# A transformer of two attentions and two expert layers on one core: routing moved ahead, blocks interleaved, the band mask moved from TensorE to VectorE

## The reference

```python
# attention A: 16 heads of 128, a band of 64 keys
h = x * rsqrt(mean(x*x) + eps) * norm_w
Q, K, V = (h @ W.T + h @ A.T @ B.T / 16 for each)      # then rope on Q and K
scores = Q @ K.T                                        # scaled; keys outside the band: -1e30
x = x + lora(softmax(scores) @ V)
# expert layer, run twice (f after attention A, g after attention B)
logits = z @ gate_w.T                                   # 16 experts
top4 = the 4 largest, weights by softmax over them
x = x + shared_mlp(z) + sum over the 4 of weight * expert_mlp(z)   # silu(z@wg.T)*(z@wu.T) @ wd.T
```

## Time and profile before

| | us |
|---|---|
| median of three runs | 1501.32 (1501.03 to 1511.45) |
| the profiled execution | 1505.28 |
| its span, first to last instruction | 1503.4 |
| PE busy | 1312.6 (87%) |
| DVE busy | 1045.4 (70%) |
| POOL busy | 870.6 (58%) |
| ACT busy | 847.9 (56%) |

### The profile page before, as it was taken

One profiled execution on the slowest core, in us unless ns is written; L12 is line 12 of the kernel. 1 busy time (PEld: TensorE's weight loads), 2 busy tenths in 40 slices (PEclk: granted clock), 3 DMA queues, 4 the chain that ended last, 5 costly groups with the idle time before them and its releaser, 6 DMA issues.

```text
span 1503.4 us, 28392 instructions
## 1 busy us (share of the span) xinstructions
PE 1312.6 (87%) x8194; PEld 1101.2 (73%) x8194; DVE 1045.4 (70%) x2274; ACT 847.9 (56%) x2102; POOL 870.6 (58%) x764
## 2 busy tenths in 40 slices
PE   5999999999988983749998989899999999978982
PEld 3888888888877883538777767677777778867872
DVE  5666666646777544438888878688888886777544
ACT  1444444454435542238778777677878875436541
POOL 3555555540346774247878777678778650356772
PEclk9999999999979997769999999999999999979996
DMA  3000000001326336221222221122222202326335
GB/s 112 26 26 26 27 25 25 16 9 55 122 84 204 109 103 213 52 58 29 59 59 63 55 68 43 43 61 63 57 69 56 57 1 77 121 92 196 103 103 178
DMA packets 58253, 110.60 MB, mean 74 GB/s; under 512 B 11456, under 2 KB 29440, under 8 KB 57856
## 3 DMA queue, kind: packets, MB, share of 16 engines
q1 hardware_dynamic: 46976, 82.11, 19.3%
q0 software_dynamic: 9024, 24.65, 5.4%
q10 hardware_dynamic: 2112, 2.10, 0.4%
HBM read 63.99 MB, written 15.47 MB: 53 GB/s over the span
## 4 chain that ended last, share of the span: by engine, by line
PE 45%; issue 19%; POOL 17%; DVE 11%; DMA 3%; ACT 2%; SPq 0%; POOLq 0%; DVEq 0%; ACTq 0%
PE ps L1450 31%; PE ps L1596 7%; POOL pb_odd L1089 4%; POOL yt L1089 3%; POOL rb L1074 2%; PE ps L1813 2%; POOL z L1089 2%; PE ps L1538 2%; POOL pb_low L1089 2%; POOL ra L1078 2%; DVE x_res L840 1%; PE ps L1673 1%; DVE pt_lo L902 1%; PE ps L1701 1%; DVE rb L541 1%
## 5 line engine op out<-in xcount | busy, mean ns | idle before, releaser
L902 DVE TENSOR_TENSOR pt_lo<-ps,pt_hi 128x512 fp32r<-128x512 f32 (+3 forms) x384 | 205.6, 548 | 54.8 <-ACT pt_hi L1369 48.4
L1450 PE MATMUL ps<-kh,qh 128*128 128x512 f32 (+3 forms) x768 | 204.1, 376 | 22.3 <-DMA qh<-qt_hi 10.2
L887 DVE TENSOR_REDUCE nmb<-ps 128x1 f32<-128x1024 f32 (+7 forms) x256 | 191.8, 749 | 29.1 <-PE ps L1450 28.1
L1369 ACT CAST pt_hi<-ps 128x512 fp32r<-128x512 f32 (+3 forms) x384 | 178.5, 481 | 58.7 <-PE ps L1813 53.1
L1450 PEld LDWEIGHTS ps<-kh,qh 128*128 128x128 f32 x768 | 132.3, 196 | 46.2 <-issue 14.3
L1450 PE MATMUL ps<-pt_hi,vst 128*128 128x512 f32 (+3 forms) x384 | 157.0, 409 | 0.9 <-DVE ra L867 0.8
L1450 PE MATMUL ps<-pt_lo,vst 128*128 128x512 f32 (+3 forms) x384 | 132.9, 350 | 0.0
L994 POOL TENSOR_TENSOR pa<-pa,rinv 128x384 f32<-128x384 f32 x64 | 52.9, 827 | 134.5 <-DVE rinv L581 134.5
L1167 ACT ACTIVATE pa<-ps,nmax 128x192 f32<-128x192 f32 x128 | 53.1, 423 | 131.0 <-DVE nmax L575 131.0
L1029 POOL DMA_INDIRECT xg<-zbuf,gidx x94 | 97.6, 1039 | 41.3 <-issue 23.8
L1089 POOL TENSOR_TENSOR pb_odd<-pb_odd,rib 128x1024 f32<-128x1024 f32 (+1 forms) x64 | 105.3, 1670 | 21.9 <-DVE rib L894 21.3
(11 more groups left out here) (222 smaller groups left out, 4219.9 us busy)
## 6 DMA issues: line engine op xcount, KB each, us to landing
raw_w<-in_wx SPq DMA_DIRECT2D x36, 608.0 KB
rb<-raw SPq DMA_DIRECT2D x192, 64.0 KB, 2.0
yg<-ybuf SPq DMA_DIRECT2D x16, 512.0 KB, 4.9
qh<-qt_hi SPq DMA_DIRECT2D x64, 128.0 KB, 2.3
qh<-qt_lo SPq DMA_DIRECT2D x64, 128.0 KB, 2.4
wa<-in_wa SPq DMA_DIRECT2D x16, 384.0 KB, 3.0
wb<-in_wb SPq DMA_DIRECT2D x8, 384.0 KB, 3.4
wo_a<-in_wo_a SPq DMA_DIRECT2D x16, 128.0 KB, 2.0
```

The costliest lines, as they stand in the source:

```text
L887: v.tensor_reduce(nmb[:, par, i:i + 1], ps[:, b:b + 2, :].rearrange("p b k -> p (b k)")[:, 0:P * (t + 1)], AX.X, ALU.max, negate=True).the ...
L902: v.tensor_tensor(pt_lo[:, s % 3, at], ps[:, 4 + s % 2, at], pt_hi[:, s % 3, at].bitcast(F32), ALU.subtract).then_inc(sem("b_pt_lo"), 1)
L1369: s_.copy(pt_hi[:, s % 3, at], ps[:, 4 + s % 2, at]).then_inc(sem("b_pt_hi"), 1)
L1450: return t_.matmul(o, l, r, start=start, stop=stop)
```

## The change

In attention A the mask matmuls go. DVE adds the mask with the maximum: for each tile one operation computes minus (scores + mask) into a new SBUF buffer `sma` and the minimum of it into `nmax`. The exponential reads `sma` with scale -1. The scores of a head's first pairs now wait for the maximum before them, no longer for the exponential.

In the expert layer the routing is issued earlier. The first norm and `logits(0)` move forward into the output projection, and `picked(0)` to its step 14. The later pieces follow two to three blocks earlier. The order of the blocks becomes: 12 shared, r0, r1, two shared, r2, r3, two shared, the rest. The conversions shift accordingly, and POOL has one fewer.

The rows of `ybuf` are laid out so that a token's four outputs are contiguous; four DMAs of two tiles each read all of it into a `yg` that holds all eight tiles. In f a conversion of attention B's value weights moves from among the additions to before them.

```diff
+FRONT = 12
+ORDER = ([("s", n) for n in range(FRONT)] + [("r", 0), ("r", 1), ("s", 12), ("s", 13), ("r", 2), ("r", 3), ("s", 14), ("s", 15)] +
+         [("r", b) for b in range(4, NB)])
-POOL_LO = 9
+POOL_LO = 8
-YG_RING = 4
+TILE_ROWS = TOPK * P + TOPK
...
-                for t in range(NT):
-                    if t >= YG_RING:
-                        sp.wait_ge(sem(f"{s}_added"), since(s, "added") + t - YG_RING + 1)
-                    first = P * (1 + TOPK * t)
-                    sp.dma_start(yg[:, t % YG_RING, :, :],
-                                 ybuf[first:first + TOPK * P, :].rearrange("(k p) e -> p k e", p=P)).then_inc(
-                        sem(f"{s}_yl{t % YG_RING}"), 16)
+                for n in range(NT // 2):
+                    sp.dma_start(yg[:, 2 * n:2 * n + 2, :],
+                                 tiles[2 * n:2 * n + 2, 0:TOPK * P, :].rearrange("t (p k) e -> p t (k e)", k=TOPK)).then_inc(
+                        sem(f"{s}_yl{n}"), 16)
...
-                v.tensor_reduce(nmax[:, 2 * n:2 * n + 2], ps[:, bank, 0:2 * KW].rearrange("p (t k) -> p t k", t=2),
-                                AX.X, ALU.max, negate=True).then_inc(sem("a_max"), 1)
+                v.memset(waited[:, :], 0.0)
+                for m in range(2):
+                    t = 2 * n + m
+                    last = v.tensor_tensor_reduce(out=sma[:, t, :], in0=ps[:, bank, KW * m:KW * m + KW],
+                                                  in1=maska[:, 0 if t == 0 else 1, :], scale=-1.0, scalar=3e38,
+                                                  op0=ALU.add, op1=ALU.min, accum_out=nmax[:, t:t + 1])
+                last.then_inc(sem("a_max"), 1)
...
                 step(0)
                 normalized(s, 1)
-                picked(0)
                 step(1)
                 norm_lo(s, 1, ACC[before][1])
                 step(2)
+                picked(s, 1)
                 step(3)
-                picked(1)
+                starts()
+                places()
+                step(4)
+                hot(0)
+                step(5)
+                hot(1)
+                step(6)
+                experts()
+                tables()
                 shifted()
...
-                    s_.activation(pa[:, t, 0:KW], ps[:, bank, KW * m:KW * m + KW], ACT.Exp,
+                    s_.activation(pa[:, t, 0:KW], sma[:, t, :], ACT.Exp, bias=nmax[:, t:t + 1], scale=-1.0,
...
                 if n < 2:
-                    after(pe, "a_exp", 4 * h + n - 1)
+                    after(pe, "a_max", 4 * h + n - 1)
...
-                    mm(o, qr[:, u, P * t:P * t + P], kr[:, u, P * t:P * t + KW], True, False)
-                    last = mm(o, idb[:, :], maska[:, 0 if t == 0 else 1, :], False, True)
+                    last = mm(o, qr[:, u, P * t:P * t + P], kr[:, u, P * t:P * t + KW])
...
-                    if h == 10:
+                    if h == 7:
                         norm(nxt, 0, 0)
+                    elif h == 11:
+                        logits(nxt, 0)
...
-ACT_HI = {0: (2,), 2: (3,), 4: (4,), 5: (5,), 7: (6,), 8: (7,), 10: (8,), 11: (9,), 13: (10,), 14: (11,),
+ACT_HI = {0: (2,), 2: (3,), 4: (4,), 6: (5,), 8: (6,), 9: (7,), 12: (8,), 14: (9,), 16: (10,), 17: (11,),
...
-DVE_LO = {12: (9,), 14: (10,), 15: (11,), 17: (12,), 19: (13,), 21: (14,), 23: (15,), 25: (16,), 27: (17,)}
+DVE_LO = {13: (8,), 15: (9,), 17: (10,), 18: (11,), 20: (12,), 21: (13,), 23: (14,), 24: (15,), 26: (16,), 27: (17,)}
```

More of the change, by code:

```diff
@@ L100, in build @@
             topf = sb("topf", [P, NT, 8], c=own)
+            ie = sb("ie", [P, NE], c=own)
             ex = sb("ex", [P, NT, TOPK], c=own)
@@ L202, in build @@
                 rinv = sb("rinv", [P, NT], c=own)
-                maska = sb("maska", [P, 2, KW], BF16, own)
+                maska = sb("maska", [P, 2, KW], c=own)
+                sma = sb("sma", [P, NT, KW], c=own)
+                waited = sb("waited", [P, 1], c=own)
             own = ExitStack()
@@ L620, in out_lo, with link_, picked @@
                                 ALU.subtract).then_inc(sem(f"{s}_ot_lo"), 1)
+            linked = {"f": 0, "g": 0}
+            def link_(s, ins):
+                linked[s] += 1
+                ins.then_inc(sem(f"{s}_route"), 1)
+                dve.wait_ge(sem(f"{s}_route"), since(s, "route") + linked[s])
+            def picked(s, half):
+                four = slice(4 * half, 4 * half + 4)
+                picks = slice(4 * half * TOPK, (4 * half + 4) * TOPK)
+                dve.wait_ge(sem(f"{s}_logits"), since(s, "logits") + half + 1)
+                link_(s, v.tensor_copy(lg[:, four, :],
+                                   ps[:, 3, 64 * half:64 * half + 64].rearrange("p (t e) -> p t e", e=NE)))
+                for t in range(4 * half, 4 * half + 4):
+                    ins = v.max(top[:, t, :], lg[:, t, :])
+                link_(s, ins)
+                for t in range(4 * half, 4 * half + 4):
+                    ins = v.max_index(topi[:, t, :], top[:, t, :], lg[:, t, :])
+                link_(s, ins)
+                link_(s, v.tensor_copy(topf[:, four, :], topi[:, four, :]))
+                dve.wait_ge(sem(f"{s}_consts"), since(s, "consts") + 32)
+                link_(s, v.tensor_tensor(hit[:, picks, :].rearrange("p (t k) e -> p t k e", t=4),
+                                     ie[:, :].unsqueeze(1).unsqueeze(1).broadcast_to([P, 4, TOPK, NE]),
+                                     topf[:, four, 0:TOPK].unsqueeze(3).broadcast_to([P, 4, TOPK, NE]),
+                                     ALU.is_equal))
+                with nc.allow_low_precision(reason="a sum of 0s and 1s, at most 4"):
+                    v.tensor_reduce(chosen[:, four, :], hit[:, picks, :].rearrange("p (t k) e -> p t e k", t=4),
+                                    AX.X, ALU.add).then_inc(sem(f"{s}_chosen"), 1)
             def out_proj(s, nxt):
@@ L644, in out_proj @@
                                         ALU.subtract).then_inc(sem(f"{nxt}_wg_lo"), 1)
-                    elif h == 12:
+                    elif h == 10:
                         norm_lo(nxt, 0, 0)
+                    elif h == 14:
+                        picked(nxt, 0)
             out_proj("a", "f")
             def ffn(s, before):
-                me = sem(f"{s}_route")
-                n = 0
                 def link(ins):
[L656 to L682, removed]
+                    link_(s, ins)
                 def shifted():
@@ L1584, in _, with logits @@
             all_pairs(pe, head_a)
+            def logits(s, half):
+                pe.wait_ge(sem(f"{s}_xt_lo"), since(s, "xt_lo") + 2 * half + 2)
+                if half == 0:
+                    pe.wait_ge(sem(f"{s}_wg_lo"), since(s, "wg_lo") + 1)
+                for t in range(4 * half, 4 * half + 4):
+                    last = three(ps[:, 3, NE * t:NE * t + NE], lambda c, a: xt(a, c, P * t, P),
+                                 lambda c, b: (wg_hi, wg_lo)[b][:, c, :])
+                last.then_inc(sem(f"{s}_logits"), 1)
             def out_proj(s, nxt):
@@ L1608, in out_proj @@
                     step(1, h)
-                    if h == 10:
+                    if h == 7:
                         norm(nxt, 0, 0)
+                    elif h == 11:
+                        logits(nxt, 0)
             out_proj("a", "f")
             def ffn(s, before):
-                def logits(half):
-                    pe.wait_ge(sem(f"{s}_xt_lo"), since(s, "xt_lo") + 2 * half + 2)
-                    if half == 0:
-                        pe.wait_ge(sem(f"{s}_wg_lo"), since(s, "wg_lo") + 1)
-                    for t in range(4 * half, 4 * half + 4):
-                        last = three(ps[:, 3, NE * t:NE * t + NE], lambda c, a: xt(a, c, P * t, P),
-                                     lambda c, b: (wg_hi, wg_lo)[b][:, c, :])
-                    last.then_inc(sem(f"{s}_logits"), 1)
                 def ranks():
@@ L2003 @@
 F_TOTAL.update({f"{kind}{u}": 16 * uses(u) for kind in ("gat", "sca") for u in range(4)})
-F_TOTAL.update({f"yl{u}": 16 * (NT // YG_RING) for u in range(YG_RING)})
+F_TOTAL.update({f"yl{n}": 16 for n in range(NT // 2)})
 def since(s, name):
```

161 lines of the change are left out of this document (77 added, 84 removed).

## The result

The changed kernel took 1516.8 us in the median of 9 runs (1512.62 to 1521.17), the kernel before 1503.82 beside it (9 runs). The ratio is 1.0083, 95% interval 1.0062 to 1.0104: slower by 0.8%. The forecast was 1513, range 1480 to 1536, with "within 1%" as the likeliest.

What follows compares the result with a forecast made beforehand. PE was taken to bound attention A, and POOL's alternating gathers and scatters the routed blocks. Attention 0, feed-forwards +14 and tail -2.5 made +11.5 on the median 1501.32: 1513 us, range 1480 to 1536.

Steps and rivals of the forecast that it cites:

- Attention A: Attention A as a whole: PE's saving and DVE's added work come out even, 0 us, ends -10 and +15.
- the price of a pair on DVE: Attention A: maximum with mask for two tiles takes DVE 0.89 us, 0.41 more than before; bounds 0.77 and 1.21.
- an excess of 0.87: Attention A: DVE's full stretch outlasts PE's by 0.87 us, a new PE wait in each of eight windows, 7 us.
- a tighter order on PE: Attention A: longer chain from the maximum and scores' bank released by DVE tighten PE's order; -3 raised to 0.
- The saving: Attention A: dropping 128 mask matmuls of 0.08 us each frees 10.2 us on PE, all on the path.
- Rival 1: Attention A: DVE becomes the bound, adding 7 to 20 us there; 1520 to 1533 us in all, chance 0.25.
- Expert layers: Both feed-forwards: PE waits before the first routed block, the fifth comes late; last scatter +7 us each, +14 together.
- r4's place: Feed-forward front: the fifth routed block's transpose on PE comes at about 472 us, 5 us late.
- the criterion that the first gather should not be before 446: Feed-forward front: first gather expected at 449 to 451 us; one before 446 would show the forecast wrong.
- Tail: Additions ending both feed-forwards: a moved conversion and removed waits save 2.5 us together, ends -6 and +2.
- Rival 2: Feed-forwards: conversions do not hold the gathers, which start at 441 us; 1477 us in all, chance 0.2.
- Rival 3: Feed-forwards: moved blocks fit inside POOL-bound time, the fifth routed block keeps its place; 1491 to 1498 us, chance 0.2.

Runs made afterwards that it cites:

- e1: The kernel before with only the mask part of the change (masked minimum on DVE, no mask matmul): 1496.34 us, ratio 0.9957.
- e8: The kernel before without mask matmuls and nothing in their place, read only in attention A: 282.1 us from first scores to last products, against 293.4.
- e2: The changed kernel with the mask back on PE, all else as changed: 1527.82 us, ratio 1.0162.
- e4: The changed kernel with block order and conversions of before, routing still early: 1498.46 us, ratio 0.9983.
- e5: The changed kernel with expert weights cast after the same steps as before, POOL still one conversion fewer: 1507.92 us, ratio 1.0032.
- e6: The changed kernel with all 16 shared blocks in front and its own later conversions: 1497.92 us, ratio 0.9957.
- e9: The changed kernel with all 16 shared blocks in front and weights cast after the steps of before, POOL one conversion fewer: 1496.88 us, ratio 0.9938.
- e7: As e5, with the casts of weights 3 to 7 one to two steps earlier still: 1500.07 us, ratio 0.9972.
- e10: As e7, with the first five routed blocks in one piece behind the 12 shared blocks: 1500.42 us, ratio 0.9957.
- e3: The changed kernel with routing, block order and conversions of before, so mask and read pass alone: 1495.00 us, ratio 0.9948.

## Why the prediction was right, and where not

The sign and the size were right (+0.8% against +0.8% in forecast, 1516.8 against 1513), but as a sum of two terms that missed in opposite directions. That they came so close together is luck. The interval leaves out 1, so these 0.8% can be told from none, which the prediction had doubted for any change under 1%.

- **Attention A: forecast 0, measured -8.2 us from the first scores to the last products in the profiled execution and -6.5 in the time of e1.** The step that failed is the price of a pair on DVE: 0.89 us was taken, with 0.77 as the lower bound; it is 0.56. Neither the accumulator read nor the memset is a step of its own in DVE's time, and even the lower bound had given each 0.07. With 0.08 instead of 0.41 more per pair, DVE's full stretch stays under PE's (10.18 us busy of 10.43), which is why PE hardly waits: 0.4 us per window, where an excess of 0.87 was forecast. The sum itself had come to -3; it was raised to 0 for a tighter order on PE, and no run shows a cost of that size. The saving was a little undersized: 11.3 us by e8 instead of 10.2. Rival 1 is out for the same reason.
- **Expert layers: forecast +7 each, measured +15.1 and +16.9 in the traces, +24 for both less the read pass in e2.** The mechanism holds: gathers held by POOL's conversions rather than by the indices, PE standing still before r0 (8.0 us; 6 were forecast), eight blocks instead of four up to r4 (19.5 us; 17.4 forecast). Its size was about half of what was measured. The sum missed two things: the alternation became 5 us longer, from casts that wait for raw weights (2 us had been added for the conversions in all), and the output projection became 4.2 us longer while the front up to r0's transpose became only 3.1 shorter. Of the 4.2, 2.7 are the logits, which only moved; the other 1.5 go with the dip of the clock, since e4, which has no dip there, has 60.3 us of projection and the changed kernel 61.8. For f that makes 4.2 - 3.1 + 8.4 (r0 to r4) + 5.2 (alternation) + 0.5 (behind it), 15.1 before rounding. e5, e6 and e9 show order and conversions as separate causes, the order as the larger.
- **r4's place**: forecast 472, read 467.17. That is absolute time; all of it starts 9 us earlier because of attention A. From the output projection's first matmul it is 137.3 us against 127.9 before, so 9.4 late where 5 were forecast. The same holds for the criterion that the first gather should not be before 446: it was at 443.78, so the sign of being wrong, as written, was there, while from the output projection's start it is 113.9 us against 112.7, no earlier. The mark should have been put in the stage's own time.
- **Tail: forecast -2.5, measured -3.3.**
- **Rival 2** (gathers start early) needed the conversions out of the way; e7 and e10 did that and still end at 1500, so in neither of these orders did it come to 1477. **Rival 3** is out: in the stage's own time r4 did not keep its place.

One thing stays open. Attention B was 7.3 us shorter in the one execution of the changed kernel than in that of the kernel before, with unchanged code. Over twelve profiled executions the same stretch runs from 634.1 to 646.3 us without regard to the part that was changed, and in the kernel before the clock was 0.97, 0.97 and 0.93 in three of its 50 us windows where the changed kernel had 1.00, 1.00 and 0.97. No run was made to separate it; I count it as scatter between executions, and so the +24 of e2, to which the read pass's 3 have to be added, is a better figure for the layers than the sum of two traces.

Six versions are faster than both kernels, by 0.3 to 0.6%, with intervals that leave out 1: e1, e3, e6, e7, e9 and e10. The lowest ratios are those of e9 (0.9938) and e3 (0.9948), but e1, which has nothing but the mask on DVE (0.9957), can't be told from them: no time here shows a gain from anything but the mask.

## What to carry to other kernels

An operation that starts earlier is worth something only if what it releases can use it: the indices came 8 us earlier in the stage's own time and stood behind POOL's conversions, and once these were moved (e7, e10), PE's order took the gain back. Where a resource is full in a long stretch (POOL's alternation), look for the event that starts the stretch and count what each engine must do before it; moving work from before it to behind it can make the full engine wait there, as POOL did in e10. Compare two traces in a stage's own time: here 9 us of every later shift came from the stage in front. An instruction's record is not what it takes from its engine: use the distance to the next start.

## What the hardware showed that was not expected

The masked minimum with its accumulator read takes DVE 0.27 to 0.28 us from start to start, though its record says 354 ns and the read's 83: two of them over 192 columns cost 0.56 us, 0.08 more than one plain reduce over 384 (0.48). Behind the small logits matmuls (128x16) inside an output projection the granted clock fell to 0.57 over 4 us, though PE was busy without a gap before and during it. It did not always: of the eight profiled executions with the logits there, four (the changed kernel, e2, e6, e9) have the dip in the first output projection, and seven, all but e2, in the second; what decides is open.
